# Causal items of a decoder layer: projection and split one slot sooner, choice of experts in two parts, gathered rows summed sooner in two

## Chip, core and metric

One core of one Trainium2 chip. The metric is the device time of one launch in microseconds (us), lower is better.

## What is computed

x is 16 sequences of 256 tokens with 128 channels. The reference applies three blocks, each followed by a layer norm:

```python
x = _layernorm(x + attn(x))          # 16 heads of 8, causal, relu projections, own norm
x = _layernorm(x + xattn(x, ctx))    # 16 heads, 64 context rows of 96 channels
x = _layernorm(x + ffn(x))
# ffn, for l in 0, 1:
x = x + _attn(_ln(x), ...)           # causal, 16 heads of 8
h = _ln(x)
x = x + moe(h)                       # l=0: each token its 2 best of 8 experts
                                     # l=1: each sequence its 2 best of 8 experts
```

An expert is 128 -> 512 -> gelu -> 128; the two best are weighted by a softmax over their logits. All is in float32.

## The kernel before

**Items.** The attention work is a list of 64 items, one per sequence and attention: 16 "self" (numbers g = 0 to 15), 16 "ctx" (16 to 31), 16 "ffn" of layer 0 (32 to 47) and 16 "ffn" of layer 1 (48 to 63). Self and ffn items are the causal ones; each has 12 rounds, a ctx item 4. Between layer 0 and layer 1 stand 46 tiles of the token experts, behind layer 1 the sequence experts.

**Slots.** Every engine walks the same time grid. `first_slot[g]` is where item g starts; a causal item comes 12 slots behind the last. Each function of an item (a stage) is a generator that starts at a slot relative to its item and goes on by one slot at each `yield`. `interleave` runs through the slots and, within a slot, through the live stages by rank and then by age, and this is the order in which an engine's instructions are written. Slots are an order and not a time: an engine runs its list as fast as its waits let it. The relative slots stand in the class `AT` (lines 59 to 71) and in the lists `sp_stages`, `pe_stages`, `act_stages`, `dve_stages`, `pool_stages`.

In the text a "slot" is counted modulo 12, from the start of the item whose scores run. A causal item's side steps on the way to its own start are, before the change:

- `sp_fetch` (slot -29, that is 7): SyncE reads x into `xin`. In layer 1 also `pool_gather` (-37 to -34, slots 11, 0, 1, 2): four indirect DMAs bring the rows of the two chosen experts into `gathered`.
- `dve_prepare`: for self items `sums` and `gone` (L961, L965) at -23 and `tok` (L974) at -21. For ffn items the norm's statistics (`norm_begin`, L899 and L905) at -24 and -23 and `tok` (L920) at -20. For layer 1 all four sums x + gate * row (L950, the combine) stand ahead of it at -25.
- `pe_transpose` and `act_source` (-19): TensorE turns `tok` (L546), ScalarE writes `srcT`.
- `pe_project` and `act_project` (-16, slot 8): queries and keys into the bank `tokens` (L563, L567), and from there to `queries_keys_taken`.
- `dve_split` (-15 and -14, slots 9 and 10): the high part (L989) and the low part (L997) of the float32 values; GpSimd copies the high part (L1210, L1211). Then SyncE spreads and stacks them through DRAM (-14 and -8).

An item's main work: in slot r TensorE makes the scores of round r (L619), VectorE takes their maxima (`negmax`, L1014 or L1018). In the slot behind the last round VectorE splits them (`maxparts`, L1033, L1035), and one slot on TensorE turns the maxima (L648) in two halves, each taken away by ScalarE (L840). From slot 17 on TensorE makes weights (L673, L678), ScalarE the exponentials (L859), GpSimd the causal mask (L1170), TensorE the values (L709, L716). `pe_outputs` and `dve_outputs` follow: denominators (L1047) in slot 8, `ao` (L1060) in slot 9, which TensorE turns in slot 10 for ffn items (L736), residual (L1105) in slot 0.

**The choice of experts.** Every item of layer 0 has a route step while the third item behind it runs: `dve_route` normalises in slots 1 and 2, and in slot 3 does the whole choice: logits, the top two, their difference (L1127), their indices (L1129), `chosen_e` (L1132), `route_hot` (L1134), `route_mask` (L1137). TensorE makes ranks from the mask (L768 to L771) in slot 5, VectorE the rows' places in slot 6.

**Experts' tiles.** `dve_out` (L1608) empties the output bank of each tile and stands on VectorE between the side steps of the first layer 1 items.

## Time and profile before

| what | value |
|---|---|
| median of 3 runs | 1322.35 us |
| lowest and highest | 1315.83, 1324.52 us |
| span of the profiled execution | 1327.3 us |
| PE, DVE, ACT, POOL busy | 92%, 70%, 61%, 54% of the span |
| chain that ended last | PE 66%, DVE 13%, ACT 4%, DMA 4% |

The profiled execution is one of its own, beside the three timed runs; its span is 4.95 us above their median. Busy shares are over the whole span. The stages have other limits each, so the rows that count are those of a stretch of one stage.

### The profile page before, as it was taken

How to read it: one execution, taken by the hardware profiler on the slowest of the kernel's cores; microseconds unless marked ns; L12 is line 12 of the kernel's file. 1: busy time of each engine (PE TensorE's matmuls, PEld its weight loads, DVE VectorE, ACT ScalarE, POOL GpSimd, SP SyncE). 2: the span in 40 equal slices, each digit the busy share in tenths (PEclk: the TensorE clock that was granted, in tenths of full speed). 3: DMA queues.
4: the chain of work that ended last, by engine and by line, in shares of the span. 5: the costliest groups of instructions: out<-in, count | busy, mean ns of one | idle time of the engine just before them, and what ended most of it. 6: DMA issues, size and time to landing. Idle time of an engine off the chain costs nothing.

```text
span 1327.3 us, 30592 instructions
## 1 busy us (share of the span) xinstructions
PE 1215.2 (92%) x9884; PEld 990.1 (75%) x9884; DVE 926.7 (70%) x2791; ACT 803.1 (61%) x1629; POOL 710.5 (54%) x1279
## 2 busy tenths in 40 slices
PE   4999999998887699999999899999999999989996
PEld 3777777766665477777777799898677777769996
DVE  6799999988777779989985221125788888635553
ACT  4566666775665366666666556564666666654552
POOL 4455555664231156777778431332677775445654
PEclk9899999998898799999998899999899999979998
DMA  4788776425666354555442787786565565255773
GB/s 118 218 230 239 221 225 185 125 71 155 167 168 163 94 141 127 128 131 136 120 118 63 225 231 232 229 254 209 140 154 146 152 155 148 79 156 166 213 201 103
DMA packets 208291, 216.94 MB, mean 163 GB/s; under 512 B 46403, under 2 KB 157507, under 8 KB 208132
## 3 DMA queue, kind: packets, MB, share of 16 engines
q1 hardware_dynamic: 191088, 193.49, 54.0%
q0 software_dynamic: 6304, 14.43, 3.9%
q10 hardware_dynamic: 10740, 7.06, 1.7%
q8 instruction: 80, 1.31, 0.4%
q14 instruction: 79, 0.65, 0.2%
HBM read 126.90 MB, written 85.46 MB: 160 GB/s over the span
## 4 chain that ended last, share of the span: by engine, by line
PE 66%; DVE 13%; issue 5%; SPq 5%; ACT 4%; DMA 4%; POOL 3%; POOLq 0%; DVEq 0%; ACTq 0%
PE scores L619 6%; PE weights L1573 6%; PE values L709 5%; PE weights L673 5%; PE scores L1831 4%; PE weights L678 4%; PE weights L1847 4%; PE values L716 3%; PE scores L1557 3%; PE scores L628 3%; DVE negmax L1014 3%; SPq L475 3%; DMA windows<-parts 2%; PE tokens L648 2%; PE tokens L582 2%
## 5 line engine op out<-in xcount | busy, mean ns | idle before, releaser
L1170 POOL TENSOR_SCALAR_AFFINE_SELECT probs<-probs 128x256 f32<-128x256 f32 (+1 forms) x576 | 279.5, 490 | 228.7 <-ACT probs L859 225.4
L859 ACT ACTIVATE probs<-weights 128x512 f32<-128x512 f32 x448 | 264.9, 598 | 120.3 <-PE weights L673 86.8
L1014 DVE TENSOR_REDUCE negmax<-scores 128x4 f32<-128x512 f32 x384 | 261.3, 685 | 86.2 <-PE scores L619 83.2
L619 PE MATMUL scores<-keys,queries 128*128 128x512 f32 (+1 forms) x384 | 186.1, 487 | 6.0 <-issue 1.7
L859 ACT ACTIVATE probs<-weights,keybias 128x512 f32<-128x512 f32 x192 | 131.5, 688 | 64.3 <-PE weights L673 48.0
L673 PE MATMUL weights<-queries,keys 104*128 104x256 f32 x768 | 159.0, 290 | 1.0 <-issue 0.6
L673 PEld LDWEIGHTS weights<-queries,keys 104*128 104x128 f32 x768 | 139.9, 194 | 22.3 <-issue 3.6
L1018 DVE TENSOR_REDUCE negmax<-scores 128x2 f32<-128x512 f32 (+1 forms) x192 | 131.0, 686 | 29.2 <-PE scores L625 19.4
L678 PEld LDWEIGHTS weights<-queries,keys 104*128 104x128 f32 x768 | 114.8, 195 | 10.2
L678 PE MATMUL weights<-queries,keys 104*128 104x128 f32 x768 | 110.2, 268 | 0.0
L709 PE MATMUL values<-probs,v 128*32 128x256 f32 x1536 | 106.6, 396 | 3.5 <-POOL probs L1170 3.5
L1573 PEld LDWEIGHTS weights<-out_room,probs 128*128 128x128 f32 x736 | 97.3, 193 | 7.3 <-DVE probs L1608 2.6
L619 PEld LDWEIGHTS scores<-keys,queries 128*128 128x128 f32 (+1 forms) x384 | 74.2, 194 | 37.6 <-issue 28.4
L1573 PE MATMUL weights<-out_room,probs 128*128 128x128 f32 x736 | 98.1, 277 | 2.2 <-DVE probs L1608 2.2
L1608 DVE TENSOR_TENSOR probs<-weights,hidden_room 128x256 f32<-128x256 f32 x46 | 19.5, 423 | 97.1 <-PE weights L1573 93.8
L1879 ACT ACTIVATE probs<-scores,out_room 128x256 f32<-128x256 f32 x128 | 53.6, 471 | 51.9 <-PE scores L1831 51.9
L648 PE MATMUL tokens<-ident_r,maxparts 128*104 128x128 f32 x384 | 55.4, 268 | 20.5 <-ACT queries L840 12.1
L1246 POOL DMA_INDIRECT routed_rows<-routed,slot_index x64 | 65.0, 1015 | 12.9 <-issue 12.9
L648 PEld LDWEIGHTS tokens<-ident_r,maxparts 128*104 128x104 f32 x384 | 44.2, 174 | 36.3 <-ACT queries L840 23.0
L1831 PE MATMUL scores<-srcT,hidden_room 128*128 128x256 f32 x256 | 69.3, 396 | 0.3 <-DMA hidden_room<-in_m_b 0.3
L716 PE MATMUL values<-probs,v 128*32 128x128 f32 x1536 | 63.2, 283 | 6.7 <-POOL probs L1170 6.1
L1847 PEld LDWEIGHTS weights<-out_room,probs 128*128 128x128 f32 x512 | 66.7, 192 | 3.2
(285 smaller groups left out, 2747.1 us busy)
## 6 DMA issues: line engine op xcount, KB each, us to landing
windows<-parts SPq DMA_DIRECT2D x192, 192.0 KB
queries<-windows SPq DMA_DIRECT2D x64, 384.0 KB
hidden_room<-in_m_w SPq DMA_DIRECT2D x78, 256.0 KB, 3.1
out_room<-in_m_w SPq DMA_DIRECT2D x78, 256.0 KB, 3.2
keys<-windows SPq DMA_DIRECT2D x192, 96.0 KB
routed_rows<-zeros SPq DMA_DIRECT2D x64, 256.0 KB, 3.6
windows<-parts SPq DMA_DIRECT2D x64, 120.0 KB
expert_rows<-probs ACTq DMA_DIRECT2D x46, 128.0 KB, 3.1
```

The lines of the kernel that those rows point to most:

```text
L619: i = pe.matmul(bank[:], queries[0:rows, s, t * P:(t + 1) * P], keys[0:rows, s::S4, half * P:(half + 1) * P], start=True, stop=True)
L648: i = pe.matmul(X[0:MREND, k * T + t * P:k * T + (t + 1) * P], maxparts[g % 2][:, t, 8 * s:8 * s + MREND], ident_r[:], start=True, stop=True)
L673: i = pe.matmul(bank[:, k * T:(k + 1) * T], keys[0:MREND, S4 * a + s, 0:P], queries[0:MREND, s, :], start=True, stop=True)
L678: i = pe.matmul(bank[:, a * P:(a + 1) * P], keys[0:MREND, S4 * a + s, P:T], queries[0:MREND, s, P:T], start=True, stop=True)
L709: i = pe.matmul(OB[32 * a:32 * a + 32, (s % 2) * T:(s % 2 + 1) * T], values[:, 0, S4 * s + a, :], place(r - 3 + 2 * (s % 2) + a // 2)[:, ( ...
L859: act.activation(probs[:, n % RING], weight_banks[n % 2][:], ACT.Exp, scale=SCALE, **bias).then_inc(exp_done.sem, 1)
L1014: i = dve.tensor_reduce(most[:, part, s, :], bank[:].rearrange("p (a k) -> p a k", k=P), AX.X, ALU.max, negate=True)
L1018: i = dve.tensor_reduce(most[:, t, s, heads], bank[:].rearrange("p (a k) -> p a k", k=P * (t + 1)), AX.X, ALU.max, negate=True)
L1170: pool.affine_select(out=block, in_=block, compare_op=ALU.is_ge, fill=0.0, base=0, pattern=[[0, heads], [1, P]], channel_multiplier=-1).th ...
L1573: i = pe.matmul(y[:, t * C:(t + 1) * C], hidden_of[j % LANES][:, c, t * P:(t + 1) * P], out_w[j % WEIGHTS][:, c, :], start=(c == 0), stop= ...
L1831: i = pe.matmul(hidden_banks[n % 3][:, k * T:(k + 1) * T], hidden_w[lane][:, e, c * P:(c + 1) * P], srcT[lane][:], start=True, stop=True)
L1847: i = pe.matmul(y_banks[e][:, t * C:(t + 1) * C], g_of[lane][:, e, c, t * P:(t + 1) * P], out_w[lane][:, e, c, :], start=(c == 0), stop=(c ...
```

## The change

Nothing is added or removed in what is computed; steps stand in other slots.

- Self and ffn items: `project` at -17 and `split` at -16 (slots 7 and 8), each one sooner. Ctx items as before.
- `dve_prepare` starts at -25 for self items (`sums` and `gone` in slot 11, `tok` in slot 4 and no longer 3) and at -26 for ffn items (statistics in slots 10 and 11, `tok` still in slot 4).
- Layer 1: the combine is a stage of its own, `dve_combine`, at -30: the first expert's rows in slot 6, the second's in slot 7. Its x is fetched at -33. For the first item, whose gather comes late, it stays at -25.
- The choice: difference in slot 3, indices to mask in slot 5, TensorE's ranks in slot 6, places in slot 7.

```diff
     gather = -37
     fetch = -29
+    combine = -30
+    statistics = -26
+    sums = -25
+    normed = -20
     prepare = -23
-    project = -16
-    split = -15
+    project = {"self": -17, "ffn": -17, "ctx": -16}
+    split = {"self": -16, "ffn": -16, "ctx": -15}
...
-            return combined + ((AT.spread, 1, sp_spread), (AT.fetch - (6 if U.kind == "ctx" else 0), 2, sp_fetch), (AT.stack, 1, sp_stack),
+            return combined + ((AT.spread, 1, sp_spread), (AT.fetch - (6 if U.kind == "ctx" else 4 if g >= 3 * B else 0), 2, sp_fetch), (AT.stack, 1, sp_stack),
...
             mixed_bank.until(gap_ready.sem, gap_ready.at(q))
-            yield from rest(3)
+            yield from rest(4)
             pe.wait_ge(mask_ready.sem, mask_ready.at(q))
...
             if g >= 3 * B:
-                dve.wait_ge(gathered_ready.sem(seq), gathered_ready.at(seq))
-                for k in range(K2):
-                    for t in range(NT):
-                        i = dve.scalar_tensor_tensor(x[:, t, :], gathered[g % LANES][:, t, k, :], gates[:, seq, t, k:k + 1],
-                                                     x[:, t, :], ALU.mult, ALU.add)
-                    if k == 0:
-                        step(i)
-                        settle(dve)
-                i.then_inc(combined.sem, 1)
-                yield
                 dve.wait_ge(combined.sem, combined.at(seq))
...
-            yield from rest(2)
+            yield from rest(AT.normed - begin_of(g) - (2 if U.kind == "ffn" else 0))
...
+        def dve_combine(dve, g):
+            x, seq = xin[g % LANES], g % B
+            dve.wait_ge(fetched.sem(g), fetched.at(g))
+            dve.wait_ge(gathered_ready.sem(seq), gathered_ready.at(seq))
+            for k in range(K2):
+                for t in range(NT):
+                    i = dve.scalar_tensor_tensor(x[:, t, :], gathered[g % LANES][:, t, k, :], gates[:, seq, t, k:k + 1],
+                                                 x[:, t, :], ALU.mult, ALU.add)
+                if k == 0:
+                    step(i)
+                    first_done = dve_steps[0]
+                    yield
+                    dve.wait_ge(dve_step, first_done)
+            i.then_inc(combined.sem, 1)
+            yield
+
+        def combine_slot(g):
+
+            return max(AT.combine, gather_slot(g) + 3)
+
+        def begin_of(g):
+
+            if g >= 3 * B:
+                return max(AT.statistics, combine_slot(g) + K2)
+            return {"self": AT.sums, "ffn": AT.statistics, "ctx": AT.prepare}[units[g].kind]
...
             dve.tensor_tensor(route_diff[:], route_top[:, :, 0], route_top[:, :, 1], ALU.subtract).then_inc(gap_ready.sem, 1)
+            yield from rest(2)
             for t in range(NT):
...
             dve.tensor_tensor(mask[:], hot[:, :, 0], hot[:, :, 1], ALU.add).then_inc(mask_ready.sem, 1)
-            yield from rest(3)
+            yield from rest(2)
             dve.wait_ge(ranks_ready.sem, ranks_ready.at(q))
...
-            return relay + ((AT.prepare - (g // B >= 2) - (g >= 3 * B), 2, dve_prepare), (AT.split, 1, dve_split), (0, 0, dve_scores),
+            if g >= 3 * B:
+                relay += ((combine_slot(g), 2, dve_combine),)
+            return relay + ((begin_of(g), 2, dve_prepare), (AT.split[U.kind], 1, dve_split), (0, 0, dve_scores),
                     (U.outputs + 1, 2, dve_outputs))
```

**Place A: VectorE in layer 0.** From the last round's maxima of an item to its fifth, before:

```order
L1014 TENSOR_REDUCE negmax<-scores 128x4
L1105 TENSOR_TENSOR res<-resid,mixed 128x256
L899 BN_STATS stats_pre<-xin 128x6 x2
L1014 TENSOR_REDUCE negmax<-scores 128x4
L905 BN_AGGR meanvar_pre<-stats_pre 128x2 x2
...
L1127 TENSOR_TENSOR route_diff<-route_top 128x2
L1129 MAX_INDEX route_index<-route_top,route_logits 128x8 x2
L1132 CAST chosen_e<-route_index 128x4
L1134 TENSOR_TENSOR route_hot<-number,chosen_e 128x32
L1137 TENSOR_TENSOR route_mask<-route_hot 128x16
L1014 TENSOR_REDUCE negmax<-scores 128x4
L920 TENSOR_SCALAR tok<-xin,meanvar_pre,rstd_pre 128x128 x2
```

and after:

```order
L903 BN_STATS stats_pre<-xin 128x6 x2
L1034 TENSOR_REDUCE negmax<-scores 128x4
L909 BN_AGGR meanvar_pre<-stats_pre 128x2 x2
...
L1147 TENSOR_TENSOR route_diff<-route_top 128x2
L1034 TENSOR_REDUCE negmax<-scores 128x4
L924 TENSOR_SCALAR tok<-xin,meanvar_pre,rstd_pre 128x128 x2
L1034 TENSOR_REDUCE negmax<-scores 128x4
L1150 MAX_INDEX route_index<-route_top,route_logits 128x8 x2
L1153 CAST chosen_e<-route_index 128x4
L1155 TENSOR_TENSOR route_hot<-number,chosen_e 128x32
L1158 TENSOR_TENSOR route_mask<-route_hot 128x16
```

The statistics have moved ahead of the last maxima, and the four steps from indices to mask from ahead of `tok` to behind it and one round of maxima.

**Place B: VectorE in the self stage.** From the residual sum (`res`) to the parts of the maxima, before:

```order
L989 CAST parts<-queries_keys_taken 128x512
L1060 TENSOR_TENSOR ao<-mixed,denom 128x128 x2
L1018 TENSOR_REDUCE negmax<-scores 128x2
L997 TENSOR_TENSOR parts<-queries_keys_taken,parts 128x2x256
L1076 SCALAR_TENSOR_TENSOR res<-ao,keeps,resid 128x128 x2
L1018 TENSOR_REDUCE negmax<-scores 128x2
L899 BN_STATS stats_post<-res 128x6 x2
L1033 CAST maxparts<-negmax 128x2x4x4
L1035 TENSOR_TENSOR maxparts<-negmax,maxparts 128x2x4x4
```

and after:

```order
L1017 TENSOR_TENSOR parts<-queries_keys_taken,parts 128x2x256
L1080 TENSOR_TENSOR ao<-mixed,denom 128x128 x2
L1038 TENSOR_REDUCE negmax<-scores 128x2
L1096 SCALAR_TENSOR_TENSOR res<-ao,keeps,resid 128x128 x2
L1038 TENSOR_REDUCE negmax<-scores 128x2
L903 BN_STATS stats_post<-res 128x6 x2
L955 TENSOR_REDUCE sums<-xin 128x2
L959 TENSOR_SCALAR gone<-sums 128x2
L1053 CAST maxparts<-negmax 128x2x4x4
L1055 TENSOR_TENSOR maxparts<-negmax,maxparts 128x2x4x4
```

Of the split, the low part (and no longer the high part) now stands ahead of `ao`, and `sums` and `gone` stand ahead of the parts of the maxima.

**Place C: VectorE in layer 1.** Before, from the high part of the split on:

```order
L989 CAST parts<-queries_keys_taken 128x512
L1060 TENSOR_TENSOR ao<-mixed,denom 128x128 x2
L1014 TENSOR_REDUCE negmax<-scores 128x4
L997 TENSOR_TENSOR parts<-queries_keys_taken,parts 128x2x256
L1014 TENSOR_REDUCE negmax<-scores 128x4
L950 SCALAR_TENSOR_TENSOR xin<-out_room,gates,xin 128x128 x4
L1024 TENSOR_TENSOR negmax<-negmax 128x16
```

and after, from the combine's first half on:

```order
L978 SCALAR_TENSOR_TENSOR xin<-out_room,gates,xin 128x128 x2
L1034 TENSOR_REDUCE negmax<-scores 128x4
L978 SCALAR_TENSOR_TENSOR xin<-out_room,gates,xin 128x128 x2
L1034 TENSOR_REDUCE negmax<-scores 128x4
L1009 CAST parts<-queries_keys_taken 128x512
L1067 RECIPROCAL denom<-mixed 128x32
L1034 TENSOR_REDUCE negmax<-scores 128x4
L1017 TENSOR_TENSOR parts<-queries_keys_taken,parts 128x2x256
L1080 TENSOR_TENSOR ao<-mixed,denom 128x128 x2
```

The combine has left the place just ahead of the parts of the maxima and stands, in halves, ahead of the split.

## Rows read from the trace of the kernel before

**Rows 1.** Self, layers 0, 1: us; busy PE, PEld, DVE, ACT, POOL; clock, DMA, GB/s
```profile
94.00:242.00 148.00, 146.42 (x1316) 115.69 (x1319) 133.90 (x378) 103.67 (x190) 87.06 (x180) 1.00 0.76 213
531.00:671.00 140.00, 128.59 (x1196) 102.48 (x1188) 127.61 (x413) 90.48 (x184) 107.15 (x176) 1.00 0.51 131
951.00:1110.00 159.00, 154.12 (x1401) 118.16 (x1401) 136.76 (x320) 106.59 (x211) 114.42 (x190) 1.00 0.61 151
```

**Rows 2.** Timeline, ScalarE, one copy per item: first and ninth in layer 0
```profile
531.37 0.59 ACT L868 COPY o<-values 128x512 f32<-128x512 f32 x1
...
671.77 0.59 ACT L868 COPY o<-values 128x512 f32<-128x512 f32 x1
```

**Rows 3.** PE's waits from 531 to 671 us: total, times, longest
```profile
PE tokens L546 <- DVE tok L920: 5.9, 8, 1.3
PE tokens L648 <- ACT queries L840: 3.4, 8, 0.4
```

**Rows 4.** The chain of waits in layer 0: start us, us, what
```profile
588.98 0.22 PE tokens L753 x2
...
589.57 0.70 DVE negmax L1014
...
596.77 0.29 DVE route_index L1129 x3
...
598.80 0.68 DVE tok L920 x2
599.52 0.44 PE tokens L546 x2
...
600.43 0.57 PE values L716 x16
```

**Rows 5.** Timeline, PE, scores of slot 5 in the same item
```profile
597.54 0.50 PE L619 MATMUL scores<-keys,queries 128*128 128x512 f32 x1
```

**Rows 6.** Line 1127 from 531 to 671 us: ns min/median/max, first and last start
```profile
L1127 DVE TENSOR_TENSOR route_diff<-route_top x8: 165/665/684, 543.9 to 667.1; 128x2 f32<-128x2 f32 x8
```

**Rows 7.** Timeline of the self stage, VectorE and PE
```profile
104.72 0.41 DVE L961 TENSOR_REDUCE sums<-xin 128x2 f32<-128x256 f32 x1
...
107.35 0.47 DVE L974 TENSOR_SCALAR tok<-xin,keeps 128x128 f32<-128x128 f32 x2
...
108.52 0.39 PE L546 MATMUL tokens<-ident,tok 128*128 128x128 f32 x2
...
118.75 0.28 DVE L1035 TENSOR_TENSOR maxparts<-negmax,maxparts 128x32 fp32r<-128x32 f32 x1
119.08 0.58 PE L648 MATMUL tokens<-ident_r,maxparts 128*104 128x128 f32 x4
```

**Rows 8.** Reads of x by the self items from 94 to 242 us
```profile
DMA to landing us min/median/max: 2.9/3.4/4.5
```

**Rows 9.** Timeline of layer 1, VectorE and PE
```profile
1034.16 0.42 DVE L989 CAST parts<-queries_keys_taken 128x512 fp32r<-128x512 f32 x1
1034.49 0.48 DVE L1060 TENSOR_TENSOR ao<-mixed,denom 128x128 f32<-128x128 f32 x2
...
1035.45 0.44 PE L736 MATMUL mixed<-ident,ao 128*128 128x128 f32 x2
1035.48 0.68 DVE L997 TENSOR_TENSOR parts<-queries_keys_taken,parts 128x512 fp32r<-128x512 f32 x1
...
1036.87 1.40 DVE L950 SCALAR_TENSOR_TENSOR xin<-out_room,gates,xin 128x128 f32<-128x128 f32 x4
...
1038.66 0.44 DVE L1035 TENSOR_TENSOR maxparts<-negmax,maxparts 128x32 fp32r<-128x32 f32 x1
...
1039.15 0.58 PE L648 MATMUL tokens<-ident_r,maxparts 128*104 128x128 f32 x4
```

**Rows 10.** The last of four gathers of an item on GpSimd's queue
```profile
1027.09 1.02 POOL L1263 DMA_INDIRECT out_room<-expert_rows,y_index  x1 [0.17 <-issue]
```

**Rows 11.** DMA queues from 1028.7 to 1029.2 us: packets, MB, share
```profile
q0 software_dynamic: 21, 0.06, 107.0%
```

14 lines of the change are left out of this document (8 added, 6 removed).

## The prediction

> **What bounds the kernel now.** First the page's busy shares: TensorE (PE) 92%, VectorE (DVE) 70%, which says that PE is the bound over the whole but hides that the stages differ. So next the busy time by stretch [rows 1], one stretch of each causal stage. In the self stage PE is busy 146.42 of 148 us: 1.6 us are left in nine items, and nothing of it can be much gained. In layer 1 it is 154.12 of 159, so 4.9 us idle in ten items, 0.49 each. In layer 0 it is 128.59 of 140, 11.4 us idle in eight items, 1.4 each, and DVE there is busy 127.61 of 140, as much as PE. Layer 0's items are eight in 140.40 us [rows 2], 17.55 each; that stage is bound by two engines that wait for each other. Who waits is in PE's waits: for `tok` 5.9 us in eight items, 0.74 each, and for ScalarE's copy of the maxima 3.4 us, 0.43 each [rows 3].
>
> The chain of waits shows how the wait for `tok` comes about [rows 4]. From 589.57, the last maxima of an item, to 599.48, the end of `tok`, the chain stays on DVE: 9.9 us without a gap. In it lie all twelve small steps of the choice. The stretch from `route_index` at 596.77 to the next maxima (they take 0.68 and end where `tok` starts, so they start at 598.12) is 1.35 us. When `tok` is there, PE starts its turn at 599.52.
>
> **Layer 0.** Two things leave the run ahead of `tok`: the 1.35 us from indices to mask, and the input's statistics, which go to slots 10 and 11 [place A's order]. With 1.35 us less, `tok` is early by more than the 0.74 us that PE waits, so that wait goes whole. PE also restarts slower after it: the two turns take 0.44 us in the chain where the same two turns without a wait take 0.22 [rows 4]. The wait is thus worth 0.74 us an item at the least, 0.74 + 0.22 = 0.96 at the most; I take the middle, 0.85.
>
> What is late next is the mask. It was made in slot 3 and used by PE in slot 5; now slots 5 and 6. Behind the waiting matmuls stand PE's scores of slot 7 and the projection, so a late mask costs PE its full delay. DVE, if free, starts the maxima of slot 5 when PE has made the scores, 0.50 us after their start [rows 5], needs 0.6 us for them and 1.35 for indices to mask: 2.45 us. PE in that time does scores and weights of slot 5, which took from 597.54 [rows 5] some 0.7, and from the turns of `tok` to the end of slot 6's values, 599.52 to 601.00, 1.5 us [rows 4]: it is at the mask after 2.2 us. So the mask is 0.25 us late. The bounds: the tiny steps take 0.17 us or 0.67, for the same two-column subtraction [rows 6], depending on what GpSimd does beside them. If two of the four stay short, 0 us late; if a third stretches, some 0.7. I take 0.3.
>
> The Trainium skill, "SBUF — State Buffer", on the shared port pair, says that a VectorE operation with two inputs in SBUF and a GpSimd operation that reads SBUF exclude each other, whole instructions long. The spread of rows 6, 165 to 684 ns for one form, agrees. It speaks against this change, since the mask's steps come to stand beside other GpSimd work and directly ahead of a PE that waits. If by this rule all four steps met such work, and not two as in the chain, the mask would be 0.5 us later still, 12 x 0.5 = 6 us in all and a time of 1320.
>
> Net for layer 0: 0.85 - 0.3 = 0.55 us an item; from 0.05 (0.74 - 0.7) to 0.96. The choice stands beside a full item 11 to 13 times; the first of them and those beside the tables' steps are as long or longer, so 12 x 0.55 = 6.6, I take 7 us gained, bounds 1 and 13.
>
> **Layer 1.** The combine is 1.40 us [rows 9] and stands just ahead of the parts of the maxima. Those end at 1039.10 and PE's turn starts at 1039.15: PE came late by what the trace has as a gap of some 0.15 us. Aggregation (0.4 us) takes its place, so the parts are ready 1 us sooner and the 0.15 goes. The projection between rounds 7 and 8 fills a gap of PE that is now open there; of the 0.49 us idle [rows 1] I count 0.1 for it. ScalarE's copy of the maxima keeps its 0.2. So 0.25 us x 12 items = 3 us, at most 0.49 x 14 = 7.
>
> What could be given back: the gather. Its last issue starts at 1027.09 in slot 2 [rows 10] and its packets run until 1029.2 [rows 11], 2.1 us later, with completion perhaps 3. The combine in slot 6 comes to its turn at about 1030.2, so it waits 0 us; price at the other end 0.5 us of DVE, which has a gap of that size in slot 7 anyway. The other is `ao`. It ends at 1034.97, and PE turns it at 1035.45: 0.48 us of slack [rows 9]. Now the low part of the split (0.68, some 0.6 net) stands ahead of it where the high part (0.42, 0.33 net) stood, and the high part delays the maxima of slot 9 by about 0.2: together 0.47. The slack is used up to the hundredth. I take no wait, 0.1 at most counted in the 3 us; the other end is a rival below.
>
> **Self stage.** PE has no idle to give, so DVE's new order can only cost. `sums` and `gone` (0.41 us and a small step, 0.5 together [rows 7]) now stand ahead of the parts of the maxima. Those end at 119.03, and PE's turn starts at 119.08 [rows 7]: it is DVE that sets that start already. Against the 0.5 stands that the high part and the denominators now lie ahead of the ninth maxima, where DVE now waits for PE, and that the residual sum may no longer meet GpSimd's copies. I work out a delay of 0 to 0.45 us, and take 0.2. `tok` moves from slot 3, where it ends at 107.82, 0.7 us ahead of PE's 108.52 [rows 7], to behind slot 4's maxima and an aggregation, 0.7 + 0.35 us later less the 0.5 that `sums` no longer takes: just in time. 13 items x 0.2 = 2.6 us lost; bounds 0 and 6. The fetch has 4 slots of 1.4 us to `sums` and 3 to the statistics of layer 0, 5.5 and 4.3 us, against 3.4 median and 4.5 at most [rows 8]: no wait in most items.
>
> **Borders.** At the entry to layer 0 the first items' statistics ask for x two slots sooner, and DVE is blocked until it comes: up to 2 us lost. At the entry to layer 1 the combine in halves lets a tile's output out 0.7 us sooner (half of the 1.40), and later items' combines leave the path to the maxima, some 1 to 2 us. At the start `tok` gains 0.5. Together 1 us gained, bounds -3 and +3.
>
> **Sum.** -7 - 3 + 2.6 - 1 = -8.4 us against the profiled execution's span of 1327.3. I have no time of that execution but the span; it is 4.95 above the median of 1322.35, and the difference is carried over to the median: 1314.
>
> **Rivals.** (a) Layer 0 frees itself wholly: the small steps stay short, the mask is in time, and PE alone bounds it. Then layer 0 gives 0.96 x 12 = 11.5 and more in the first items, say 13, layer 1 gives 5, the self stage costs 1, borders 2: -19, so 1303. For it speaks that DVE's load per slot becomes even; against it that DVE is as busy as PE [rows 1] and half of the small steps stretch [rows 6].
>
> (b) The wait moves and nothing is won: the mask is late by 0.7 us an item, PE waits there as it did for `tok`, and the self stage pays 0.45. Then -1 - 2 + 6 - 1 = +2, so about 1322 to 1324. The change would do what it says and the time stay. For it: DVE's sum in layer 0 is 127.61 of 140 whatever the order.
>
> (c) The other side: `ao`. From the moment that it comes more than 0.48 us later than now, PE waits in slot 10 in every ffn item, 32 in all. With 0.5 us beyond that, by a gather that lands late or a stretch of the low part beside GpSimd's copies, this is 28 full items x 0.5 = 14 us. Against it stand the 8.4 gained: +5.6, so 1328. Against this rival: GpSimd's copies come one slot after the high part, as now, and DVE is let off before slot 8.
>
> (d) The change does nothing, since slots are only an order: excluded by the order's rows, which differ at all three places.
>
> **Chances and range.** Forecast 0.48, (a) 0.27, (b) 0.16, (c) 0.09, (d) none. Within 1% of 1322.35 is 1309.1 to 1335.6, and that is about what a measurement can tell from no change, the three runs being 0.66% apart. The forecast's own range is 1307 to 1320, a fifth of it below 1309.1 (0.1); of (a) four fifths are (0.2). Of (c) a third lies above 1335.6, with waits twice as long. So faster 0.3, same 0.67, slower 0.03. The range that holds 8 in 10 reaches from (a) to (b), 1301 to 1325.
>
> **What would show it.** Right: in layer 0 PE's wait for `tok` gone and a wait of 0.1 to 0.5 us for `route_mask` in its place, eight items in some 136 us; in layer 1 no wait for `maxparts` and ten items in some 156.5 us where the stretch of rows 1 has 159; in the self stage a short wait of PE for `maxparts`, 0.1 to 0.4 us. Wrong: waits of PE for `ao` (rival c), of DVE for the gather or for x in every item, or a layer 0 whose items take 17.4 us still.

## The result, and the profile after

The changed kernel takes 1340.8 us (median of 4 runs, 1334.98 to 1344.1), where the kernel before took 1320.08 beside it: a ratio of 1.015, 95% interval 1.0113 to 1.0187. It is slower by 1.5%; 1314 was forecast. The profiled execution took 1344.1 us, its span 1342.5 us, 15.2 above the span before. One execution of a kernel below, combine_mid, took 3724.44 us, far outside all others, and stands in no ratio.

The first view is the busy time by stretch, with the same columns as [rows 1]: the self stage, layer 0, a piece of the end of layer 0, layer 1, and the last item.

```profile
96.00:249.00 153.00, 148.05 (x1323) 115.88 (x1318) 134.65 (x379) 104.20 (x189) 85.84 (x180) 1.00 0.72 206
537.00:678.00 141.00, 126.76 (x1200) 101.68 (x1192) 127.98 (x412) 89.49 (x185) 107.65 (x177) 1.00 0.52 131
696.00:716.00 20.00, 18.38 (x149) 14.47 (x149) 13.60 (x42) 10.44 (x21) 12.17 (x20) 0.83 0.20 54
959.00:1107.00 148.00, 138.03 (x1252) 105.85 (x1255) 119.11 (x288) 96.33 (x190) 102.99 (x171) 1.00 0.57 145
1182.00:1202.00 20.00, 18.01 (x135) 12.63 (x131) 7.36 (x45) 8.71 (x20) 8.01 (x16) 0.61 0.58 163
```

PE idles 4.95 us in 153 of self stage, where [rows 1] had 1.58 in 148; in layer 0 it idles 14.2 of 141 (before 11.4 of 140), in layer 1 10.0 of 148 (before 4.9 of 159). In none of them does PE idle less than before.

ScalarE's copy of `o` comes once in an item, so its starts are a ruler, and "an item" below is the time from one such copy to the next. In the timeline of the changed kernel they stand, for the twelfth item of the self stage, the two copies of [rows 2] in layer 0, the last of layer 0 and the first of layer 1, at:

```profile
249.61 0.59 ACT L872 COPY o<-values 128x512 f32<-128x512 f32 x1
...
537.56 0.59 ACT L872 COPY o<-values 128x512 f32<-128x512 f32 x1
...
678.72 0.58 ACT L872 COPY o<-values 128x512 f32<-128x512 f32 x1
...
748.33 0.58 ACT L872 COPY o<-values 128x512 f32<-128x512 f32 x1 [3.26 <-PE values L720]
...
958.98 0.60 ACT L872 COPY o<-values 128x512 f32<-128x512 f32 x1
```

Against the same copies before (242.47, 531.37, 671.77, 736.76, 951.04) they are later by 7.1, 6.2, 7.0, 11.6 and 7.9 us; the last copy of all is 15.7 later. So the self stage lost 7 (1.3 of them ahead of its first copy), the stretch from there to the middle of layer 0 as good as nothing, layer 0's end 5; the border to layer 1 gave 3.6 back, and layer 1 lost 8. The item itself went from 16.50 to 17.03 us in the self stage, from 17.44 to 17.36 in layer 0, and in layer 1 from 15.91 to 15.88, but with four items of 16.6 to 18.1.

PE's waits say on what (total us, times, longest), first in the self stage (96 to 249 us), then in layer 0 (537 to 642 us), then in layer 1 (959 to 1107):

```profile
PE tokens L652 <- DVE maxparts L1055: 3.6, 9, 0.4
```
```profile
PE values L720 <- POOL probs L1193: 4.8, 6, 0.8
...
PE mixed L772 <- DVE route_mask L1158: 1.7, 7, 0.3
```
```profile
PE mixed L740 <- DVE ao L1080: 4.4, 4, 1.5
PE tokens L652 <- ACT queries L844: 3.8, 9, 0.4
```

In these 105 us of layer 0 the wait for `tok` of [rows 3] is gone, and the mask is late by 0.24 us each time. Over the eight items of [rows 3], from 537 to 678 us, it comes back in the last two:

```profile
PE tokens L550 <- DVE tok L924: 1.6, 2, 0.8
```

And a wait for GpSimd's causal mask, 0.8 us an item, stands in layer 0, and waits for `ao` in layer 1. The first of these has a forerunner in the view of [rows 3] that the rows leave out:

```profile
PE values L716 <- POOL probs L1170: 0.9, 3, 0.4
```

### The profile page after: what moved, and what is told of

The parts are those of the page before. It is cut to its first block, busy times and chain, and to the rows that moved or that the text cites. A ratio compares the mean times of both kernels' runs of the same rounds, so it can differ in the third digit from the quotient of the medians.

```text
span 1342.5 us, 30596 instructions
## 1 busy us (share of the span) xinstructions
PE 1220.8 (91%) x9884; PEld 992.9 (74%) x9884; DVE 917.2 (68%) x2791; ACT 802.1 (60%) x1629; POOL 710.7 (53%) x1279
## 4 chain that ended last, share of the span: by engine, by line
PE 59%; DVE 15%; issue 7%; POOL 6%; SPq 5%; DMA 4%; ACT 4%; POOLq 0%; DVEq 0%; ACTq 0%
PE weights L1600 6%; PE scores L623 6%; PE scores L1858 4%; PE values L713 4%; PE weights L1874 4%; PE weights L677 4%; PE weights L682 3%; SPq L479 3%; PE scores L1584 3%; PE values L720 3%; DMA windows<-parts 2%; POOL probs L1193 2%; PE tokens L567 2%; DVE negmax L1038 2%; DVE negmax L1034 2%
## 5 line engine op out<-in xcount | busy, mean ns | idle before, releaser
L1193 POOL TENSOR_SCALAR_AFFINE_SELECT probs<-probs 128x256 f32<-128x256 f32 (+1 forms) x576 | 282.5, 497 | 259.1 <-ACT probs L863 256.4
L623 PEld LDWEIGHTS scores<-keys,queries 128*128 128x128 f32 (+1 forms) x384 | 74.4, 195 | 28.3 <-issue 15.6
```

Source lines behind the costliest of these rows:

```text
L623: i = pe.matmul(bank[:], queries[0:rows, s, t * P:(t + 1) * P], keys[0:rows, s::S4, half * P:(half + 1) * P], start=True, stop=True)
L1193: pool.affine_select(out=block, in_=block, compare_op=ALU.is_ge, fill=0.0, base=0, pattern=[[0, heads], [1, P]], channel_multiplier=-1).th ...
```

## The experiments

All are made from the changed kernel, and all times are ratios to the kernel before on the same chip (95% interval); 0.001 is 1.3 us. A "back" is a part undone. Theories and rivals A, B and C are those of the expectation just above. Item times, waits and borders are from one profile of each kernel.

**First four: one part undone.** self_back sets the self stage's slots to those of before:

```diff
-    sums = -25
-    normed = -20
-    project = {"self": -17, ...
-    split = {"self": -16, ...
+    sums = -23
+    normed = {"self": -21, "ffn": -20}
+    project = {"self": -16, ...
+    split = {"self": -15, ...
```

> Only the self stage goes back to its old order: projection and split at -16 and -15, sums and gone at -23, tok at -21; layers 0 and 1 stay as changed. Theory A (the loss is three costs in three places, and the self stage's is PE's wait for maxparts, 0.42 us in each item of 17.03): the self items return to 16.5 us, the wait of PE's turn for maxparts is gone, and the time falls by 6 to 7 us, from 1340.8 to about 1334. Rival B (the self stage's longer items are the price of something that lies in the later stages too, such as TensorE's granted clock or DMA load of the day): the self items stay near 17 us and the time within 2 us of 1340.8.

Measured: 1.009 (1.0054 to 1.0125); self items of 16.49 us, and no wait of PE in the view of the self stage. Theory A.

combine_back takes out the yield between the halves and sets the combine to -25, the statistics to -24, the fetch to -29, in layer 1 only; the border below is the time from the last copy of `o` in layer 0 to the first in layer 1.

> Only layer 1 goes back: its combine in one piece at -25, its statistics at -24, its fetch at -29; the earlier projection and split stay. Theory A (VectorE reaches the combine in slot 6 before the gathered rows have landed, stands there 0.4 to 3 us, and its ao comes late for TensorE): the waits of VectorE for the gather go, the four items of 16.6 to 18.1 us go back to about 15.9, and the time falls by 5 to 9 us, to about 1333. Rival B (it is the split's low part ahead of ao that delays ao, whatever the combine does): PE's waits for ao, 4.4 us in 959 to 1107, stay at over 3 us, and the time falls by less than 3 us.

Measured: 1.0144 (1.0096 to 1.0192), so not shown to be faster, where A had forecast 5 to 9 us. Layer 1's items were 15.95 us with none longer than 16.3, and no wait for the gather, as A said; but the border to layer 1 took 215.3 us where the changed kernel has 210.7. What layer 1 wins, 4.7 us without its last item, is spent at the border.

choice_back gives VectorE's and PE's rests of the choice back; split_back sets projection and split to -16 and -15 for both kinds.

```diff
             dve.tensor_tensor(route_diff[:], ...
-            yield from rest(2)
...
             dve.tensor_tensor(mask[:], ...
-            yield from rest(2)
+            yield from rest(3)
...
-            yield from rest(4)
+            yield from rest(3)
             pe.wait_ge(mask_ready.sem, ...
```

> Only layer 0's choice is in one part again, with the mask in slot 3 and its ranks in slot 5; statistics two slots sooner and the projection one sooner stay. Theory A (the time of layer 0's items is held by a ring of waits, so that one wait's going only lets the next one decide, now TensorE's 0.83 us for GpSimd's causal mask): items of 17.3 to 17.6 us in the middle of layer 0 and a wait for tok of under 0.5 us; the end of layer 0, where items are 5 us longer than before, gets 0 to 4 us back; time 1337 to 1342. Rival B (the choice in two parts is what pays in layer 0, and the early statistics alone do not): items of 17.8 us and more, and the time rises by 3 to 6 us, to about 1345.

> Only the projection and the split go back by a slot, in the self stage and in both layers; sums, statistics, choice and combine stay as changed. Theory A (in the self stage it is sums and gone, 0.57 us, standing ahead of maxparts that makes it late): PE's wait for maxparts stays at 0.3 us or more in each self item, and the self stage gains under 2 us. Rival B (the high part, standing ahead of the ninth maxima, is what delays that chain): the self items return to 16.5 us, 6 us gained there. In layer 1, if the low part ahead of ao costs what the prediction feared, PE's waits for ao fall by more than half although VectorE still waits for the gather. By A the time is 1337 to 1343, by B about 1331.

Measured: choice_back 1.0228 (1.0184 to 1.0271), layer 0 items of 18.1 us: rival B. PE waits there for GpSimd (4.1 us in five items) and for `tok` (3.2). So the choice in two parts saves 0.75 us an item here, in a layer that as a whole gained 0.1: something else in it costs. split_back 1.0143 (1.0096 to 1.019), theory A: self items 17.2 us, so the sums ahead of `maxparts` are the self stage's cost, and the earlier split had softened it by 0.2; layer 0 items 17.18, so there the earlier split costs 0.18 an item. In layer 1 (957 to 1107 us) PE's waits for `ao` fell from 4.4 us to 1.9, although VectorE still waited 12.1 us for the gather: by the test of the expectation the low part of the split ahead of `ao` has a share in that wait.

**Moves on GpSimd and of the statistics.** gather_sooner has `gather = -41`; statistics_back has layer 0's statistics at -24; scatter_two yields after two scatters; mixed_one puts together what the first four seemed to recommend, as its expectation lists.

> Only the gather's four issues are moved, 4 slots (5.3 us) sooner, from -37 to -41; the combine stays in two halves at -30 and -29. Theory A (what VectorE waits for at the combine is the landing of the last gathered rows, 2.8 us after its issue's end in most items and up to 4.8 us in some): with 5.3 us more there is no wait of VectorE for the gather in the stretch of layer 1's middle items, the items of 16.6 to 18.1 us are gone, and the time falls by 5 to 8 us, to about 1334. Rival B (the halves of the combine in slots 6 and 7 make ao late by their own 1.4 us of VectorE, whether they wait or not): the waits for the gather go, but PE's waits for ao stay at over 2 us in ten items and the time falls by less than 3 us. Rival C (the issues, at 1 us of GpSimd each, now stand ahead of causal masks that TensorE is waiting for): items of over 16.2 us with waits of PE for GpSimd.

Measured: 1.0219 (1.0162 to 1.0276). Waits for the gather and for `ao` gone, but every layer 1 item 16.6 us: rival C. From its timeline, GpSimd and the matmul that waits:

```profile
1032.23 0.97 POOL L1290 DMA_INDIRECT out_room<-expert_rows,y_index  x1 [0.16 <-issue]
...
1033.21 0.64 POOL L1193 TENSOR_SCALAR_AFFINE_SELECT probs<-probs 128x512 f32<-128x512 f32 x1
...
1033.90 0.65 PE L720 MATMUL values<-probs,v 128*32 128x128 f32 x16 [0.63 <-POOL probs L1193]
```

The issue of an indirect transfer (0.97 us) stands ahead of the mask that PE's values of slot 0 want. The changed kernel's layer 0 has the same picture with a scatter:

```profile
596.47 1.01 POOL L1269 DMA_INDIRECT routed_rows<-routed,slot_index  x1 [0.17 <-issue]
...
597.49 0.65 POOL L1193 TENSOR_SCALAR_AFFINE_SELECT probs<-probs 128x512 f32<-128x512 f32 x1
...
598.19 0.65 PE L720 MATMUL values<-probs,v 128*32 128x128 f32 x16 [0.82 <-POOL probs L1193]
```

> Only the statistics of layer 0's input are back at -24 (layer 1 keeps its own); the choice stays in two parts. It was choice_back that showed items of 18.1 us, 0.7 us longer than before the change. Theory A (statistics two slots sooner put 1 us of VectorE ahead of maxparts and ao, and only the choice in two parts pays for it; undone, VectorE's run ahead of tok is long again but without indices and mask): layer 0's items take 17.0 to 17.3 us, the time falls by 1 to 4 us, to about 1338. Rival B (the early statistics are needed, because with them late tok is late again even without the 1.35 us of indices and mask): a wait of PE for tok of 0.3 us or more, items of 17.5 us and more, and the time rises by 1 to 5 us.

Measured: 1.0134 (1.0074 to 1.0194), layer 0 items 17.47 us: as the changed kernel within the interval. Neither theory came about: no item of 17.3 or less as A said, no wait for `tok` as B said; PE waited for GpSimd as in the changed kernel. But the entry to layer 0, from the last copy of the ctx stage to the first of layer 0, took 29.8 us where the changed kernel has 31.7.

> Only GpSimd's four scatters of layer 0 are moved: two in slot 8 and two in slot 9, instead of one in each of the slots 8 to 11. Theory A (the 0.83 us that PE waits in slot 0 of each item for a causal mask comes from the scatter, 1.0 us, that stands directly ahead of that mask): this wait goes or falls under 0.3 us, and the items shorten from 17.35 to 16.6 to 17.1 us, unless the pairs make masks of slots 9 and 10 late by as much; time 1330 to 1338. Rival B (the mask is late because ScalarE's weights come late, not because GpSimd is taken): the wait stays at 0.6 us or more, and so do the items and the time.

Measured: 1.0664 (1.0605 to 1.0723), most items of 23.7 us. PE's wait in slot 0 is not shorter but longer, 14.7 us in five items. Layer 0's middle by busy time, and PE's wait there:

```profile
567.00:686.00 119.00, 103.11 (x750) 82.48 (x746) 71.09 (x245) 55.98 (x116) 66.82 (x110) 0.77 0.37 96
```
```profile
PE values L720 <- POOL probs L1193: 14.7, 5, 3.0
```

Theory A's place was right (what stands ahead of that mask decides) and its gain wrong: the second pair now stands there, 2.3 us from the start of its first issue to the end of its second, where one issue took 1.0. The wait grew by 2.1 us an item, the item by 6.3. Most of the difference is PE's own busy time, 20.6 us an item (103.11 in five) where the changed kernel has 15.8 (126.76 in eight): the granted clock was 0.77 of full, a mean of stretches at 2.4 and at 1.2 GHz, where the changed kernel had 1.00 with its wait of 0.8.

> A version to beat both: the self stage as before the change; in layer 0 the choice in two parts and the early statistics, but projection and split at -16 and -15; in layer 1 the combine in two halves at -28 and -27 and the gather at -39, so 4 slots more between them. If the costs found so far add (self stage 7 us, layer 0 0.17 us an item by the later projection, layer 1 5 to 8 us by the wait for the gather): 1340.8 - 7 - 2 - 6 = 1326, and with TensorE's clock less low in the last item some 1322; it would be level with the kernel before (1319). If they hang together, so that the gather moved costs GpSimd time that others wait for, 1330 or more.

Measured: 1.0073 (1.0037 to 1.0108): better than the changed kernel, and slower than the one before. Layer 1 items 16.4 us, with waits of PE for `maxparts` and GpSimd.

**One part alone.** self_sums undoes only sums, gone and tok of the self stage; split_only undoes all but projection and split; combine_later is the kernel before with layer 1's combine in halves at -28 (statistics and fetch there as changed); mixed_two is combine_later with the change's choice and statistics.

> In the self stage only sums, gone and tok go back (-23, -21); projection and split stay one slot sooner there as everywhere. Known so far: all undone gives self items of 16.49 us, nothing undone 17.03, only projection and split undone 17.25. Theory A (sums and gone ahead of maxparts are the whole cost, 0.76 us an item, and the earlier split gives some 0.2 us back): self items of 16.3 to 16.5 us, no wait for maxparts, and 7 us or more gained on the changed kernel, to 1.008 or less of before. Rival B (the earlier split only helps when something else is late, and costs when nothing is): items of 16.6 us or more, with a wait of PE in them.

Measured: 1.0067 (1.0036 to 1.0098), self items 16.42 us. A: with the earlier split in place the sums cost 0.6 us an item; the earlier split gains 0.07 without the sums.

> Everything is undone but the projection and the split, which stay one slot sooner in the self stage and in both layers. Theory A (the part that the prediction counted with 0.1 to 0.25 us an item gains nothing, because PE's turn then waits for ScalarE's copy of the maxima instead): layer 1 items of 15.9 us, layer 0 items of 17.3 to 17.6 us, 1.00 of before within 0.4%. Rival B (TensorE's projection fills a gap): items of 15.7 us or less in layer 1, 0.997 or less. Rival C (the low part ahead of ao costs PE waits for ao in layer 1, as the prediction's slower case had it): items of 16.2 us and more there with such waits, and 1.005 or more.

Measured: 1.0053 (1.0021 to 1.0085), and none of the three: layer 1 15.95 us, self 16.42, but layer 0 18.03 us, 0.6 more than before. From the timeline of the kernel before (ScalarE, GpSimd and the matmul that takes the last mask), and below it from split_only's, the same place of an item:

```profile
585.04 0.60 ACT L859 ACTIVATE probs<-weights 128x512 f32<-128x512 f32 x1 [0.20 <-PE weights L673]
585.70 0.41 POOL L1170 TENSOR_SCALAR_AFFINE_SELECT probs<-probs 128x256 f32<-128x256 f32 x1 [0.39 <-ACT probs L859]
...
586.28 1.08 POOL L1246 DMA_INDIRECT routed_rows<-routed,slot_index  x1 [0.17 <-issue]
586.35 0.47 ACT L807 ACTIVATE queries_keys_taken<-tokens,l_bq 128x256 f32<-128x256 f32 x1 [0.71 <-PE tokens L567]
...
590.25 0.63 POOL L1170 TENSOR_SCALAR_AFFINE_SELECT probs<-probs 128x512 f32<-128x512 f32 x1
...
590.93 0.64 PE L716 MATMUL values<-probs,v 128*32 128x128 f32 x16
```
```profile
585.18 0.48 ACT L811 ACTIVATE queries_keys_taken<-tokens,l_bq 128x256 f32<-128x256 f32 x1 [0.59 <-PE tokens L571]
...
585.56 0.47 ACT L815 ACTIVATE queries_keys_taken<-tokens,l_bk 128x256 f32<-128x256 f32 x1
...
585.91 0.60 ACT L863 ACTIVATE probs<-weights 128x512 f32<-128x512 f32 x1
...
586.58 0.41 POOL L1190 TENSOR_SCALAR_AFFINE_SELECT probs<-probs 128x256 f32<-128x256 f32 x1 [1.51 <-ACT probs L863]
...
587.16 1.08 POOL L1266 DMA_INDIRECT routed_rows<-routed,slot_index  x1 [0.17 <-issue]
...
590.79 0.64 POOL L1190 TENSOR_SCALAR_AFFINE_SELECT probs<-probs 128x512 f32<-128x512 f32 x1
...
591.49 0.64 PE L720 MATMUL values<-probs,v 128*32 128x128 f32 x16 [0.84 <-POOL probs L1190]
```

Before, ScalarE makes the exponentials of that slot first and the two copies of the projection after it. With the projection a slot sooner the copies (0.85 us together) come first, and the exponentials (585.91) and GpSimd's mask come after them. From that mask on GpSimd runs without a gap worth naming, scatter, copies, mask, scatter, until the mask that PE's values want. GpSimd waits 1.51 us for ScalarE at its start instead of 0.39, which is 1.12 more. From that first mask to the last the run of before has a gap of 0.39 and takes 4.55 us, that of split_only 4.21. So the last mask comes 0.8 us later, and PE waits 0.84 us for it.

> The kernel before with one part of the change alone: layer 1's combine in two halves, with its statistics at -26 and fetch at -33, but the halves at -28 and -27, two slots later than the change has them, and the gather at its old place, -37. Theory A (the gather lands 3.8 us after its last issue begins, 5.8 us at times, so that two slots more, 2.6 us, are enough nearly always, and the halves let the border to layer 1 go 4 us faster, as every kernel with halves shows it): layer 1 items of 15.9 to 16.0 us without a wait of VectorE for the gather, 210 to 212 us from the last copy of layer 0 to the first of layer 1 where before has 214.28, and a ratio of 0.995 to 0.999. Rival B (the halves in slots 8 and 9 stand ahead of maxparts, as in the kernel with gather at -39, whose items took 16.4 us): items of 16.2 us or more and a ratio of 1.002 or more.

Measured: 1.0017 (0.999 to 1.0043): rival B's items of 16.43 us with waits of PE for `maxparts` (3.3 us in nine), and a border of 209.1 us, a little better than theory A's. The two cancel.

> As the kernel combine_later, but with layer 0 as the change has it (choice in two parts, statistics at -26), with projection and split at -16 and -15. The difference of the two is what layer 0's part of the change is worth. Theory A (a steady layer 0 gains 0.1 to 0.25 us an item, 1 to 3 us, and loses about as much beside the tables' steps at its end): within 3 us of combine_later. Rival B (it costs): 4 us or more above combine_later; rival C (it pays, and the loss of the profiled run there was TensorE's clock alone): 3 us or more below.

Measured: 1.0084 (1.0056 to 1.0112), 0.0067 (8.9 us) above combine_later: rival B.

**Layer 0 and layer 1 by themselves.** choice_only, choice_stats, combine_only and choice_self_split are the kernel before with one or two parts of the change, as their expectations say.

> The kernel before with one part of the change alone: layer 0's choice of experts in two parts (indices to mask two slots later, PE's rest one slot longer); statistics, projection and split stay where they were. Theory A (the prediction's own layer 0 term holds for this part by itself: the wait for tok, 0.74 us an item, goes and a late mask takes 0.2 to 0.3 back; what spoilt it was the projection one slot sooner, whose two copies on ScalarE, 0.85 us, delay GpSimd's run of masks and scatters): layer 0 items of 16.9 to 17.2 us where before has 17.3 to 17.45, no wait of PE for GpSimd in slot 0, a ratio of 0.994 to 0.999. Rival B (layer 0 is a ring in which each wait removed hands over to another, so no part of it gains): items of 17.3 us or more and a ratio of 1.000 or more. Rival C (as the kernel mixed_two beside combine_later hints, choice and statistics cost at the end of layer 0, where the tables' steps run): steady items shorter, but a ratio of 1.003 or more.

Measured: 1.0009 (0.9983 to 1.0035). The steady items are 17.18 us, as A said, with a new wait of 0.45 us an item for the bank `mixed`, which the ranks hold until VectorE has read them (`taken`). PE's waits from 530 to 634 us:

```profile
PE mixed L732 <- DVE taken L1162: 2.7, 6, 0.5
...
PE values L720 <- POOL probs L1191: 1.7, 2, 1.2
PE mixed L772 <- DVE route_mask L1156: 1.4, 5, 0.3
```

Twelve items of 0.27 us less are 3 us that the time doesn't show, and the profiles say where they may go. The item from 542.33 us took 18.4 us, with a wait for GpSimd of 1.2; three other kernels with this choice and the old place of layer 0's projection (choice_stats, choice_self_split, split_back) have the same item at 17.9 to 18.5 us, with such a wait of 0.8 to 1.3; mixed_one and mixed_two have not. And at the end of layer 0, where before there is no wait for `tok` to save, the new waits stand all the same. The third item from the end took 16.25 us where before has 15.22, with PE's waits from 686 to 702 us:

```profile
PE mixed L772 <- DVE route_mask L1156: 0.5, 1, 0.5
PE mixed L732 <- DVE taken L1162: 0.4, 1, 0.4
```

The item behind it takes 15.6 us for 14.4 where both have full clock (choice_self_split and before). That is 2.2 us in two items. The granted clock adds to it in one run or another: here the item of 18.9 us had 0.91 and one of 20.1 us near the end too.

> As choice_only, with layer 0's statistics at -26 as well, all that the change does to layer 0 but for projection and split. Theory A (the early statistics add nothing once the choice is in two parts, their 1 us only stands elsewhere): within 0.2% of choice_only. Rival B (they put 1 us ahead of maxparts and of the run that ends on tok and the mask): 0.3% or more above choice_only. Rival C (they clear the place ahead of tok): 0.3% or more below.

Measured: 1.0039 (1.0016 to 1.0062), 0.0030 above choice_only: rival B's number, though the difference is not clear of the two intervals. The steady items are 17.18 us here too. What the profiles show is the entry to layer 0: 34.1 us from the last ctx copy to the first of layer 0, where choice_only has 32.2, and PE's wait for `maxparts` in it is 2.6 us for 1.8. The changed kernel against statistics_back shows the same 1.8 us. Further, one item near the end took 20.9 us for 17.6, with a wait of PE for `maxparts` of 0.56 us that choice_only lacks and a granted clock of 0.84; split_back and mixed_one have that item at 21.0 to 21.1, mixed_two, at full clock, at 18.2.

> The kernel before with layer 1's part of the change alone: combine in two halves at -30 and -29, statistics at -26, fetch at -33, gather at -37; projection and split as before. Theory A (the wait of VectorE for the gather costs 3 to 8 us in a few items, the border gives 2 to 4 back): a wait of VectorE for the gather of 0.3 us and more in every item, and in two to five items of 0.8 to 3 us, which are 0.5 to 2.5 us longer; 1.001 to 1.005 of before. Rival B (without the earlier projection VectorE comes to the combine later and the waits are gone): no items over 16.2 us and 0.999 or less. Rival C (the earlier projection has no part in the loss of layer 1, the halves all of it): 1.006 or more.

Measured: 0.9991 (0.9964 to 1.0018). Theory A's waits (10.1 us of VectorE for the gather in ten, at most 3.2; items of 16.5, 18.2, 16.4 and 16.5 us), and a border of 206.9 us instead of 214.3, more than A gave it: it comes out even.

> Choice_only with the self stage's projection and split one slot sooner (sums and tok there as before), the one other part that has been seen to gain: self items of 16.42 instead of 16.50 us in two kernels. Theory A (gains in different stages add): 1 us below choice_only, a ratio 0.001 lower, and the candidate to beat both kernels. Rival B (the entry to the ctx stage or the clock takes it back): the same as choice_only or above, with an entry item of 17.64 instead of 16.3 us at the end of the self stage, as in the two kernels with that split.

Measured: 1.0019 (0.9994 to 1.0043); self items 16.42, an entry item, the last but two of the self stage, of 17.46 us (choice_only 16.29). This looks like rival B, but A's gain of 0.001 is below what the intervals can tell.

**Between the two places of the combine.** `combine = -29`, all else of combine_only; and the same with the self stage's earlier split.

> The kernel before with layer 1's part alone, but the halves of the combine at -29 and -28, in slots 7 and 8, between combine_only (6 and 7: 15.85 us items with some of 16.4 to 18.2, 0.9991) and combine_later (8 and 9: 16.43 us in every item, 1.0017). Theory A (the gather's landing costs what comes too early, the place ahead of maxparts costs what comes too late, and one slot, 1.3 us, takes away the usual wait of 0.4 to 0.6 us but not those of 1 to 3 us): layer 1 items of 15.9 us with at most two longer ones, 0.996 to 0.999. Rival B (the half in slot 8 already stands ahead of the maxima whose parts PE waits for): items of 16.1 to 16.4 us, 1.000 to 1.002.

Measured: 0.9982 (0.9954 to 1.001). Layer 1 items 15.84 us with one of 16.5, border 207.9 us: theory A. Its waits from 960 to 1116 us, PE's and VectorE's:

```profile
PE tokens L652 <- ACT queries L844: 4.0, 10, 0.4
PE mixed L740 <- DVE ao L1080: 0.5, 1, 0.5
```
```profile
DVE xin L978 <- DMA table<-expert_rows,y_index: 0.7, 1, 0.7
```

The waits for the gather are gone but one. By its profile this is the best of the three places; the interval still holds 1.

> Combine_mid with the self stage's projection and split one slot sooner (self items of 16.42 instead of 16.49 us, sums and tok as before): the parts that gain, together. Theory A (they add): 1 us below combine_mid, 0.995 to 0.998 of before, faster than both kernels. Rival B (the self stage's 1 us is given back at the entry to the ctx stage, as choice_self_split, no faster than choice_only, says): the same as combine_mid or up to 2 us above it.

Measured: 1.0001 (0.997 to 1.0032): not below combine_mid, within the intervals. B's reason isn't borne out: the entry item took 15.09 us with the earlier split here and 17.15 in combine_mid without it. No kernel here is shown to beat the one before; combine_mid is the nearest.

## Why the prediction was wrong, step by step

The forecast was -8.4 us, and +20 was measured. Differences of ratios, times some 1321 us: combine -1 (combine_only), choice +1 (choice_only), statistics +4 (choice_stats less choice_only), projection and split +7 (split_only), sums and tok of the self stage +11 (the changed kernel less self_sums). Together +22; measured +20. Each is uncertain by 3 to 6 us, so that they add so well is in part luck. The items of layer 0 show that not all of them do: the earlier split costs 0.6 us an item alone (split_only) and 0.18 beside the choice in two parts (split_back); the choice saves 0.27 alone (choice_only) and 0.75 beside the earlier split (choice_back). Taken out of the changed kernel the parts give 8 us (self_back), 1 (split_back), 1 (combine_back) and -10 (choice_back).

**Self stage, forecast +2.6.** The step that failed is the term "13 items x 0.2": it is 0.53 an item (17.03 for 16.50), 7 us at the twelfth item. The place was right, the timeline shows it:

```profile
121.31 0.40 DVE L955 TENSOR_REDUCE sums<-xin 128x2 f32<-128x256 f32 x1
...
121.74 0.17 DVE L959 TENSOR_SCALAR gone<-sums 128x2 f32<-128x2 f32 x1
...
121.82 0.18 DVE L1053 CAST maxparts<-negmax 128x32 fp32r<-128x32 f32 x1
122.03 0.19 DVE L1055 TENSOR_TENSOR maxparts<-negmax,maxparts 128x32 fp32r<-128x32 f32 x1
...
122.28 0.58 PE L652 MATMUL tokens<-ident_r,maxparts 128*104 128x128 f32 x4 [0.42 <-DVE maxparts L1055]
```

From the sums' start to that of `maxparts` it is 0.51 us. Without the earlier split the sums cost 0.7 us an item (split_back 17.2 for self_back 16.5); what the rest over 0.51 is, isn't shown. I set savings against it (less waiting of VectorE, no meeting with GpSimd's copies) that are worth 0.2 at most (17.03 for 17.2); the residual sum `res`, which I hoped would shorten, took 1.09 us at 119.30 where it had 1.12. `tok`, "just in time", cost PE no wait. With DVE setting that turn to the hundredth [rows 7], the full 0.5 should have stood in the sum, 6 us, which I had as the upper bound.

**Layer 0, forecast -7.** The step as put, "that wait goes whole" and a mask 0.3 us late, came true in the first six items of the stretch, to 0.06 us. The prediction also weighed a rule of the Trainium skill ("SBUF — State Buffer", "Who interferes with whom", on the shared port pair), and from rows of its own a mask 0.8 us late if all four steps met such work. The trace shows 0.24: the steps got shorter at their new place, not longer. `route_hot` took 0.42 us at 597.57 before, with GpSimd's `routed` beside it (596.71 to 598.29), and takes 0.19 at 589.34 now, when GpSimd's mask has ended (589.28). That agrees with the rule; the meeting that I feared didn't come. What failed is the net, "0.55 us an item": it is 0.08 (17.36 for 17.44). Three sizes were wrong.

- The choice alone brings 0.27. The bank `mixed` is held until VectorE has read the ranks, now in slot 7, and PE waits 0.45 us an item for it (choice_only); the sum had no such term.
- The restart of PE, for which I took 0.11 us and at most 0.22, was misread. The 0.22 of [rows 4] is a piece of the two turns: the timeline has them at 0.38 us, and the turns of `tok` at 0.44 with the wait and 0.38 without (choice_only). So it is 0.06.
- The projection and split, which I priced in layer 1 and the self stage, were left out here. They take 0.18 us an item (17.36 for 17.18 in split_back), and 0.6 where the choice is in one part, by ScalarE's order and GpSimd's run. That chain was in none of my rows: GpSimd was 24% idle there [rows 1], and the 0.9 us of waits for its mask were in the view of [rows 3] and not in the rows that I took.

-0.27 and +0.18 leave a gain of 0.09, as measured. And counting "12 x 0.55" was wrong at the end of layer 0, where there is no wait for `tok` to save and the new waits cost 2.2 us in two items. Rival (b), the wait moves and nothing is won, describes layer 0, by other waits than the one it names.

**Layer 1, forecast -3.** "The parts are ready 1 us sooner and the 0.15 goes": it went, and PE's wait for ScalarE's copy of the maxima, of which I had written that it "keeps its 0.2", grew from 0.20 to 0.42 us an item, so the item is 15.88 for 15.91 and not 0.25 less. The other step that failed is that of the combine, "it waits 0 us". The last issue and the combine, twice:

```profile
1006.12 1.01 POOL L1290 DMA_INDIRECT table<-expert_rows,y_index  x1 [0.17 <-issue]
...
1011.95 0.61 DVE L978 SCALAR_TENSOR_TENSOR xin<-table,gates,xin 128x128 f32<-128x128 f32 x2 [2.99 <-DMA table<-expert_rows,y_index]
...
1023.98 1.01 POOL L1290 DMA_INDIRECT out_room<-expert_rows,y_index  x1 [0.16 <-issue]
...
1027.82 0.61 DVE L978 SCALAR_TENSOR_TENSOR xin<-out_room,gates,xin 128x128 f32<-128x128 f32 x2 [0.63 <-DMA out_room<-expert_rows,y_index]
```

From the issue's start to the combine it is 3.84 us in a usual item and 5.83 in a bad one; I had taken 2.1 for the packets [rows 11] and "perhaps 3" to the end, from one item. From 959 to 1107 us VectorE waited nine times, 10.5 us in all:

```profile
DVE xin L978 <- DMA table<-expert_rows,y_index: 6.0, 3, 3.0
DVE xin L978 <- DMA out_room<-expert_rows,y_index: 4.5, 6, 1.2
```

Behind the long ones `ao` is late. So the mechanism of rival (c), "a gather that lands late", came about, in four items and not in 28; the low part of the split ahead of `ao`, which it also names, has a share (split_back). Without such a wait `ao` is in time, as forecast (15.95 us in split_only, 15.84 in combine_mid).

**Borders, forecast -1.** The early statistics cost 1.8 us at the entry to layer 0, as "up to 2 us lost" had it, but VectorE has no wait for x there, and the earlier projection gives 2.0 back (changed kernel 31.7 us, split_back 33.7), so that the entry took 31.7 us before and after. The border to layer 1 gave 3.6 us; with the halves and the split of before it gave 7.4 and 6.4 (combine_only, combine_mid). That is why layer 1's part is even in the time. The border isn't the halves' alone (split_only, with the combine in one piece, has 211.6), and what else shortens it is open. The sign was right, the size too small.

**What the profile adds by chance.** Of the 15.2 us between the spans 2.2 lie in the last item, and some 3 in one item at the end of layer 0. In both the granted clock had fallen, to 0.61 and 0.83 in the two windows of 20 us of the first fence above. The kernel before, the changed one with the self stage undone, and the changed one with combine undone at the end of layer 0 show:

```profile
1169.00:1187.00 18.00, 15.82 (x124) 11.20 (x121) 6.94 (x42) 8.86 (x21) 8.46 (x16) 0.73 0.63 180
```
```profile
1174.00:1189.00 15.00, 12.13 (x119) 8.63 (x119) 6.16 (x35) 8.00 (x20) 7.73 (x15) 0.92 0.65 199
```
```profile
697.00:713.00 16.00, 14.79 (x144) 11.76 (x144) 12.32 (x40) 9.71 (x21) 11.78 (x20) 1.00 0.26 67
```

The last item took 17.20 us at 0.73, 14.92 at 0.92 and 19.42 at 0.61; an item at the end of layer 0 took 19.3 at 0.83 and 16.25 at 1.00. With the same order in layer 0 that item took 19.3 to 19.6 us in three kernels (changed, self_back, gather_sooner) and 16.2 in two (combine_back, self_sums). One profile per kernel can't give such places to the change.

The chance of 3% for slower by over 1% was too low. The self stage's 0.2 and the gather's 0 were taken near their favourable end, while the slower end of each stood in its bounds or in a rival; the split's and the bank's price in layer 0 stood nowhere.

## What to carry to other kernels

Where an engine already sets a start to the hundredth, count what is put ahead of it at its full length, as the self stage showed; set nothing against it that isn't a row. Read a view of waits to its end: a short wait of today can be the long one after the change. When a step moves, follow it on every engine it issues on, in every stage it runs in: here two copies of ScalarE passed one exponential and so shifted GpSimd's gapless run. Price a part beside the other parts too: the same move cost 0.6 us an item alone and 0.18 with them. And count a gain only in the items that have the wait it takes away. A transfer's landing is to be read as a spread over many items (start of the issue to the first use that waited), and an engine that blocks on it in order needs the long end, not the median.

## What was unexpected of the hardware

- A longer wait can cost more than itself. With PE waiting 0.8 us an item for GpSimd the granted clock stayed at 1.00; with 2.9 us an item (scatter_two) it was 0.77 on average and the item 6.3 us longer for 2.1 us more wait.
- In 118 runs of the kernel before, from 1311.7 to 1332.3 us, the time went with the mean granted clock of the run (0.942 to 0.969): a straight line through them falls by 7.3 us for each 0.01. Most of what one run differs from the next goes with this (the correlation is -0.89), so differences of 3 us between single runs mean nothing. Which causes which isn't shown.
- Kernels with the same order of instructions in layer 0 have different steady items there: 17.18 us in split_back and 17.34 in mixed_one; 17.44 in the kernel before and 17.28 in combine_later; 17.36 in the changed kernel and 17.49 in self_sums. In the first pair the difference stands in PE's wait at its turn of the maxima, 0.43 us an item in split_back and 0.59 in mixed_one, though every engine's list is the same there. What outside that list makes it is open.
